# A two-layer graph network on one core: layer 0's row loop written out for all 49 iterations

## What is computed

```python
h = relu(layernorm(x))                       # layer 0: attention, 4 heads of 32
e = (h @ W_embed);  z = (e.a_src)[src] + (e.a_dst)[dst];  logit = leaky_relu(z, 0.2)
p = softmax of logit over the edges of one dst
x = x + segment_sum(e[src] * p, dst) + h @ W_lin + bias
h = relu(layernorm(x))                       # layer 1: messages
m = relu(concat(h[src], h[dst], bond) @ W1 + b1) @ W2 + b2
x = x + segment_sum(m * sigmoid(bond @ Wa + ba), src)
```

## Time and profile before

| | |
|---|---|
| profiled execution | 1536.59 us, its span 1534.6 us |
| median of the runs | 1535.7 us (1535.42 to 1541.37) |
| busy: POOL, DVE, PE, ACT | 1139.4, 1100.7, 1021.9, 782.2 us |
| layer 0's gathers | from 14.44 to 542.26 us |
| first send of the sums | 596.69 us |
| granted clock, mean | 0.87 |

### The profile page before, as it was taken

The page is one execution under the profiler, slowest core; times in us unless marked ns, Lnnn a source line. Parts: engine busy times, 40 slices in busy tenths (PEclk is TensorE's granted clock), DMA queues, the critical chain, the costliest instruction groups (busy, mean ns, idle before and its releaser), DMA issues.

```text
span 1534.6 us, 23152 instructions
## 1 busy us (share of the span) xinstructions
PE 1021.9 (67%) x5651; PEld 760.7 (50%) x5651; DVE 1100.7 (72%) x3786; ACT 782.2 (51%) x2168; POOL 1139.4 (74%) x992
## 2 busy tenths in 40 slices
PE   0777777777777764655554477667777677677663
PEld 0555565655655544555554344444545444454442
DVE  2889898989889888988888655555555556555551
ACT  0788888888888885666655322222222222222220
POOL 5777777777777713777777668888888888888884
PEclk9999999999999985767776689898898899889996
DMA  8477777777777744555554333333333333333332
GB/s 268 129 215 215 223 212 221 213 219 227 214 227 214 222 161 152 180 179 171 173 174 152 97 47 50 49 50 52 50 50 51 52 50 52 50 50 50 50 40 21
DMA packets 177809, 202.28 MB, mean 132 GB/s; under 512 B 22219, under 2 KB 130767, under 8 KB 177599
## 3 DMA queue, kind: packets, MB, share of 16 engines
q1 hardware_dynamic: 119421, 122.80, 24.8%
q0 software_dynamic: 56496, 71.62, 24.7%
q10 hardware_dynamic: 1810, 6.93, 1.4%
HBM read 90.62 MB, written 109.84 MB: 131 GB/s over the span
## 4 chain that ended last, share of the span: by engine, by line
POOL 40%; issue 27%; DMA 20%; DVE 8%; PE 2%; ACT 1%; POOLq 0%; SPq 0%; DVEq 0%; ACTq 0%
POOL out_dram L1169 17%; POOL XE L1155 8%; DMA out_dram<-BD,sx 7%; POOL out_dram L1115 4%; POOL O L443 3%; POOL XN L443 3%; POOL R L443 3%; POOL XE L443 3%; DMA O<-in_x_dram,ix 2%; DMA XE<-in_x_dram,ix 2%; DMA R<-in_x_dram,ix 2%; DMA XE<-out_dram,ixs 2%; DMA out_dram<-BS,sx 2%; DMA XN<-in_x_dram,ix 2%; DVE H L889 1%
## 5 line engine op out<-in xcount | busy, mean ns | idle before, releaser
L1115 POOL DMA_INDIRECT out_dram<-BD,sx x196 | 205.2, 1047 | 115.2 <-issue 60.8
L1155 POOL DMA_INDIRECT XE<-out_dram,ixs x196 | 209.0, 1066 | 62.0 <-issue 57.4
L1269 DVE TENSOR_SCALAR XN<-bank,bwc 128x128 f32<-128x128 f32 x196 | 55.2, 344 | 270.8 <-PE bank L1396 270.8
L715 ACT ACTIVATE BD<-BD,nmr,rstd 128x128 f32<-128x128 f32 x392 | 170.8, 488 | 67.7 <-DVE nmr L576 67.7
L1169 POOL DMA_INDIRECT out_dram<-BS,sx x100 | 160.1, 1601 | 42.6 <-issue 35.9
L1054 PE MATMUL bank<-BD 128*128 128x128 f32 x392 | 110.6, 377 | 120.5 <-DVE BD L932 120.5
L1169 POOL DMA_INDIRECT out_dram<-TS,sx x96 | 153.7, 1601 | 37.3 <-issue 27.6
L1377 PE MATMUL bank<-ident,XE 128*128 128x128 f32 x196 | 40.8, 344 | 190.4 <-DMA XE<-out_dram,ixs 190.4
L777 PE MATMUL bank<-ident,BD 128*128 128x128 f32 x588 | 108.2, 295 | 80.0 <-DVE BD L569 77.9
L1054 PEld LDWEIGHTS bank<-BD 128*128 128x128 f32 x392 | 87.0, 274 | 131.4 <-issue 131.4
L789 PE MATMUL bank<-wes,TS 128*128 128x132 f32 x392 | 101.1, 341 | 71.0 <-ACT TS L726 68.5
(11 more groups left out here) (229 smaller groups left out, 3246.8 us busy)
## 6 DMA issues: line engine op xcount, KB each, us to landing
out_dram<-BD SPq DMA_DIRECT2D x98, 512.0 KB, 3.0
base_rows<-BD SPq DMA_DIRECT2D x49, 256.0 KB, 3.8
BD<-base_rows SPq DMA_DIRECT2D x49, 256.0 KB, 3.5
H<-BD SPq DMA_DIRECT2D x49, 256.0 KB, 3.2
XE<-in_x_dram SPq DMA_DIRECT2D x13, 512.0 KB, 6.6
BD<-bond_rows SPq DMA_DIRECT2D x49, 128.0 KB, 2.1
bond_rows<-in_edge_attr_dram ACTq DMA_DIRECT2D x1, 6250.0 KB, 23.6
XN<-in_x_dram SPq DMA_DIRECT2D x12, 512.0 KB, 6.1
```

The source lines that it names most:

```text
L715: last = nc.scalar.activation(OT[u][:, g, w:w + D], OT[u][:, g, w + D:w + 2 * D], ACT.Relu, bias=nmr[:, slot, t:t + 1], scale=rstd[:, slot ...
L1115: pool.indirect_dma_start(out, bass.IndirectOffsetOnAxis(sx[:, u, c:c + 1], 0), RO4[u][:, c, :], None, bounds_check=lim, oob_is_err=False) ...
L1155: pool.indirect_dma_start(XS4[u][:, c, :], None, halves, bass.IndirectOffsetOnAxis(ixs[:, u, c:c + 1], 0), bounds_check=lim, oob_is_err=Fa ...
L1269: last = nc.vector.tensor_scalar(MS[:, c * D:(c + 1) * D], bM[:, c * D:(c + 1) * D], bwc[:, u % 2, c:c + 1], None, ALU.mult)
```

## The change

`loop4` is removed, and the five engines' row functions call `every4`, which was there already for the later stages:

```diff
-        def loop4(eng, body):
-            for it in range(4):
-                body(it, it, 0)
-            with eng.Fori(1, ITS // 4 - 1) as i:
-                for u in range(4):
-                    body(4 * i + u, u, i)
-            for it in range(4 * (ITS // 4 - 1), ITS):
-                body(it, it % 4, it // 4)
-
         def every4(eng, body):
             for it in range(ITS):
                 body(it, it % 4, it // 4)
...
-            loop4(pool, body)
+            every4(pool, body)
...
-            loop4(sp, body)
+            every4(sp, body)
...
-            loop4(dve, body)
+            every4(dve, body)
...
-            loop4(act, body)
+            every4(act, body)
...
-            loop4(pe, body)
+            every4(pe, body)
```

## The result

The written-out kernel is slightly faster. Its median is 1534.5 us over 17 runs (1528.1 to 1538.3), that of the kernel before beside it 1538.75 us over 17 runs (1533.3 to 1544.3). The ratio is 0.9968, with a 95% interval of 0.9956 to 0.9981, so some 5 us are gone. A second measurement gave 0.9972 (0.9954 to 0.9990). The forecast was 1538 us, 0.15% slower than the 1535.7 us known then; the interval lies wholly on the other side of no change.

A forecast was written before the change was run, and what follows sets the result against it. GpSimd's gathers were taken to bound layer 0, with DVE waiting for them. Profiled 1536.59 us + 0 (branches) + 0 (registers) + 2.5 (code) = 1539.1, less 0.9 to the runs' median: 1538 us, range 1531 to 1545.

The forecast's parts named there:

- register arithmetic: Layer 0 loop: register-compared waits and dynamic addresses become constants; taken as 0, ends 6 us faster and 6 us slower.
- lower end: Layer 0, register removal: all overlap of gathers with L564 disappears, 0.15 us for 40 iterations, 6 us faster.
- Moved: nothing.: All queues: the order on each stays, SP's stores and loads included; no time was given to it.
- SP has no part in the chain: SP's queue in the loop: SP waits for DVE and does not affect the chain; no time given.
- Code fetch: Layer 0 loop: 15 and 23 added instruction packets, some 40 with SP's; 2.5 us slower, ends 0 and 5.
- The delay of a landing: Behind a group's last gather: a packet between issue and landing makes the landing 0.33 us later, 15 of 40 packets.
- starved: Rival, layer 0: each of 40 added packets stops the gather stream, 25 us, 1561 us; chance 0.10 together with fuller overlap.
- Back edges at nothing: Loop ends: removing 10 compare-and-branches per engine gains nothing; 0.5 us on POOL if the cover were gone.
- phase leaves the overlap: Rival, layer 0: DVE passes L564 and L597 between gathers, up to 14.0 us goes, 1523 us; chance 0.09.
- The tail: After layer 0's last gather: iterations 45 to 48 and the softmax, already written out, stay unchanged at 54.43 us.
- the first send: Start of the second stage: the first send was expected near 599 us if the forecast was right.

The follow-up runs named there:

- dve_only: The kernel before with only DVE's queue written out, the other four engines keeping the loop; ratio to the kernel before 1.0011.
- all_but_sp: All engines written out except SP, which keeps the loop of the kernel before; ratio to the kernel before 0.9985.
- sp_late_b: The written-out kernel with SP alone made late again by added semaphore increments before its stores, spills and loads; ratio to the kernel before 0.9979.
- one_input_b: The written-out kernel with L564 and L597 reading one input instead of two, leaving out two parts of the computation; ratio to the kernel before 0.9945.
- sp_only: The kernel before with only SP's queue written out, the other four engines keeping the loop; ratio to the kernel before 0.9990.

## Why the prediction was wrong

**The step that failed** is "register arithmetic": "I take 0, because the wait for the landing re-sets DVE's phase in every iteration, and L597 follows it by operations that hold no register work". Its lower end, that the overlap with L564 disappears, came in part: of 5.2 us of hold under L564, 3.0 went, and of 9.8 under L597 1.6, which is about the whole of the 4.5 (means of three and four profiles). The second half of the reason was right: from the read of the last column to L597 it is 2.47 us (median) in every one of these profiles. The first half wasn't enough: the wait for the landing does re-set DVE's phase, but to the landing, and that has itself moved against the gathers, from 4.1 us behind the last one to 3.5 to 4.0, and spread out. From L597 to L564 DVE needed 4.04 us in each of three profiles before and 3.99 or 4.00 in each of four after. So the part that I had priced is 0.04 us. It goes straight into the hold, since L564 ended only 0.25 us into a gather (median), but it isn't enough by itself: dve_only gained 1 to 2 us. What the runs show is that the whole of the gain in layer 0 lies in which operation starts first, and that moving one instruction by some 0.25 us with the loop in place gives 3.1 of the 4.5. Which engines' timing moves the landing isn't settled; no single one gives the gain.

**"Moved: nothing."** The order stayed, but not the time. SP's store after L597 was issued 0.18 us behind its end before (171.12 + 0.67, then 171.97) and 0.03 us after (170.30 + 0.67, then 171.00):

```profile
171.97 0.37 SPq L468 DMA_DIRECT2D out_dram<-BD  x1
```

```profile
170.30 0.67 DVE L588 TENSOR_TENSOR BD<-BD 128x512 f32<-128x512 f32 x1
...
171.00 0.37 SPq L459 DMA_DIRECT2D out_dram<-BD  x1
```

"SP has no part in the chain" was right of waits and wrong of timing: all_but_sp keeps the excess at 17.1, sp_late_b loses half of the gain.

**Code fetch.** The count was right: 16 and 24 more packets, 15 and 23 forecast for the loop's stretch. The delay of a landing was nearly right as well, which the prediction had from two cases: in the four profiles after, an instruction packet fell into the 2.5 us behind a group's last gather in 75 of 160 iterations (47%, where 38% were forecast for a slightly longer time), and DVE read the last column 3.97 us behind that gather there, against 3.61 in the other 85, so 0.36 us later (forecast 0.33). That is a correlation and no experiment; sp_late_b has 0.02 us, one_input_b 0.80. What failed is that half of this reaches GpSimd (2.5 us): the holds in the iterations with a packet are no longer than in those without, 0.20 against 0.24 us. The pauses of GpSimd are unchanged to 0.1 us in all. The rival "starved" (1561 us) is refuted by the same pauses.

**Back edges at nothing** was right: no pause between gathers of the kernel before is longer than 0.31 us, at the ten edges or elsewhere, and with L564 moved, the stretch with a loop is 524.9 and without one 525.3. The rule of the Trainium skill's Runtime: NRT & Kernel Launch ("Instruction fetch mechanics") that speaks for unrolling would have had the sign right for another reason; no run here shows a stall at this loop's edge.

**What held:** GpSimd bounds layer 0, gathers 1.3 to 1.35 us apart with 391 pauses of 0.30, DVE with 1.1 us of air per iteration, holds as the only variable, later stages unchanged within their scatter. **What was mis-weighed:** the rival "phase leaves the overlap" (1523, chance 0.09) was the right mechanism at a third of its size: 4.5 of 14 us. I had demanded that both operations move by 0.2 to 0.3 us; L564, which met a gather in 37 to 40 of 49 iterations and ended 0.25 us into it, needs less. The measured 1534.5 us lies inside the stated range of 1531 to 1545, but that is owed to its width: the sum behind the forecast has the wrong sign. The tail, forecast at 54.4 us, was 52.7 (53.3 in the mean of four against 54.1), and the first send came at 590.2, not near 599.

## What to carry to other kernels

Where GpSimd's indirect DMAs bound a stage, subtract their usual unhindered length from each: the excess here was the time in which DVE's operations with two SBUF inputs held them, and it hung on which one started first, so an edit that shifts a queue by 0.1 to 0.3 us can pay or cost several us. Don't price such a shift at zero because a wait re-sets the phase: take the distance between the operation and the gather from the rows, and if it is smaller than what any engine may move, give the case without overlap a chance of its own. And compare stages over three profiles, not spans of one: here the gain of 4.5 us stood out in its stage, where a kernel repeats within 1.2 us at most, and was invisible in the span.

## What the runs showed that I had not expected

A one-input operation of 128x512 in 0.41 us holds a gather, at its beginning by up to 0.34 us and near its end by 0.22, where a 128x128 one with two scalar operands does not. A gather often waits through two successive holding operations (18 of 24, once 0.60 us over a seam of 0.08), and sometimes slips in between. A last column that can be read 1.2 us sooner (sp_only, 2.9 in place of 4.1 us) can make the gather stream longer, by 1.5 us. An instruction packet behind the last gather went with a read 0.36 us later, without longer holds. And chips differ: on one, with a granted clock of 0.80 in layer 0, GpSimd waited for DVE and DVE for PE, and the kernel took 1716 us; a variant that is 0.26% faster elsewhere was 1.8% faster there.
